# A transformer layer in split fp32 on one Trainium2 core: places and order of weight sums, two loads moved, a doubled half chunk

## The reference, cut to what matters

```python
mod = (silu(c) @ wmod).reshape(4, 6, 1, 1024)          # sa, ca, ga, sb, cb, gb
h = layernorm(x) * (1 + ca) + sa                       # x: 4 x 512 x 1024
x = x + ga * (h @ (weight * block_mask).T)             # attention stand-in, 1024 x 1024
h = layernorm(x) * (1 + cb) + sb
w1, w2, w3 = nf4_table[q] * scale                      # scale by 64 inputs
y = (silu(h @ w1.T) * (h @ w2.T)) @ w3.T               # hidden 2752 = 21 chunks of 128 and one of 64
x = x + gb * y
```

## Time and profile before

| what | value |
|---|---|
| median of 3 runs | 1547.49 us (1547.21 to 1549.31) |
| profiled execution | 1548.19 us, its span 1546.5 us |
| TensorE, VectorE, ScalarE busy | 97%, 73%, 61% of the span |
| DMA queue of SP | 67.8% of 16 engines |
| plain chunks, pass 1 | about 259 to 328 us, 332 to 702 us |
| pass 2, down projection | about 702 to 1123.5 us, 1123.5 to 1542.4 us |

### The profile page before, as it was taken

How to read it: one execution, slowest core, us unless ns; L and a number is a source line. 1 busy time by engine, 2 the same in 40 slices (tenths; PEclk the granted TensorE clock), 3 DMA queues, 4 the chain that set the end, 5 groups by cost and what they waited for, 6 DMA issues and landing times.

```text
span 1546.5 us, 19239 instructions
## 1 busy us (share of the span) xinstructions
PE 1498.0 (97%) x6984; PEld 1232.5 (80%) x6984; DVE 1133.5 (73%) x1751; ACT 942.6 (61%) x1091; POOL 5.5 (0%) x10
## 2 busy tenths in 40 slices
PE   4899999989999999999999999999899999999998
PEld 3687888777888888888888888888688888888887
DVE  5687786798888898888655565656665767956894
ACT  3465677799999999834868677782333433332320
POOL 0000000000000000000000000000000000000000
PEclk9999999999999999999999999999899999999999
DMA  9976444766666666655567777775686878857973
GB/s 366 367 262 232 155 141 154 248 209 228 222 214 205 217 211 198 202 187 178 188 207 243 229 230 238 232 229 192 227 303 251 313 235 309 324 172 269 400 275 119
DMA packets 188191, 362.78 MB, mean 235 GB/s; under 512 B 15392, under 2 KB 82368, under 8 KB 187072
## 3 DMA queue, kind: packets, MB, share of 16 engines
q1 hardware_dynamic: 181760, 358.39, 67.8%
q10 hardware_dynamic: 6336, 3.15, 0.7%
HBM read 258.16 MB, written 103.32 MB: 234 GB/s over the span
## 4 chain that ended last, share of the span: by engine, by line
PE 80%; DVE 8%; DMA 7%; ACT 2%; issue 2%; SPq 1%; DVEq 0%; ACTq 0%
PE ps L2290 15%; PE ps L2291 15%; PE ps L2292 15%; PE ps L2363 9%; PE ps L2361 9%; PE ps L2362 9%; PE ps L2196 2%; PE ps L2198 2%; PE ps L2197 2%; DMA weight_piece<-wT 1%; PE ps L2151 1%; DMA wmod<-wmod 1%; ACT w_raw L1046 1%; DMA xm_d<-modulated 1%; DMA x_d<-x_extra 1%
## 5 line engine op out<-in xcount | busy, mean ns | idle before, releaser
L2290 PE MATMUL ps<-x_m_hi,up_weight_hi 128*128 128x512 f32 x972 | 381.7, 393 | 15.4 <-ACT up_c L1276 7.2
L2291 PE MATMUL ps<-x_m_lo,up_weight_hi 128*128 128x512 f32 x972 | 380.6, 392 | 0.0
L2292 PE MATMUL ps<-x_m_hi,up_weight_lo 128*128 128x512 f32 x972 | 380.4, 391 | 0.0
L1046 ACT ACTIVATE w_raw<-w_raw 128x2048 f32<-128x2048 f32 (+1 forms) x145 | 271.9, 1875 | 3.5
L2361 PE MATMUL ps<-t_hi,s_hi 128*128 128x512 f32 x616 | 239.6, 389 | 0.0
L2362 PE MATMUL ps<-t_lo,s_hi 128*128 128x512 f32 x616 | 239.6, 389 | 0.0
L2363 PE MATMUL ps<-t_hi,s_lo 128*128 128x512 f32 x616 | 239.6, 389 | 0.0
L2290 PEld LDWEIGHTS ps<-x_m_hi,up_weight_hi 128*128 128x128 f32 x972 | 183.6, 189 | 55.8 <-DVE up_weight_lo L1507 10.3
L1369 ACT ACTIVATE s_hi<-s_raw 128x1408 fp32r<-128x1408 f32 x56 | 77.4, 1383 | 239.6 <-DVE s_raw L1986 191.6
L2292 PEld LDWEIGHTS ps<-x_m_hi,up_weight_lo 128*128 128x128 f32 x972 | 183.9, 189 | 38.7
L2291 PEld LDWEIGHTS ps<-x_m_lo,up_weight_hi 128*128 128x128 f32 x972 | 183.8, 189 | 37.7
(11 more groups left out here) (150 smaller groups left out, 1960.3 us busy)
## 6 DMA issues: line engine op xcount, KB each, us to landing
s_raw<-h_d SPq DMA_DIRECT2D x96, 704.0 KB, 5.7
up_weight_raw<-t_d SPq DMA_DIRECT2D x150, 256.0 KB, 5.2
wmod<-wmod SPq DMA_DIRECT2D x12, 2048.0 KB, 15.8
t_d<-up_weight_raw SPq DMA_DIRECT2D x91, 256.0 KB, 3.0
t_raw<-w_d SPq DMA_DIRECT2D x88, 256.0 KB, 6.4
w_codes<-w12q SPq DMA_DIRECT2D x41, 512.0 KB, 5.0
w_d<-w_raw SPq DMA_DIRECT2D x22, 512.0 KB, 3.9
t_raw<-w_d SPq DMA_DIRECT2D x22, 512.0 KB, 8.5
```

Source lines behind the costliest of these rows:

```text
L1046: act.activation(RAW2[n % 2][:, cols], RAW2[n % 2][:, cols] if j else RQ2[n % 2][:, cols], ACT.Prelu, bias=bias, scale=sign, alpha=slope). ...
L2290: pe.matmul(acc, th[:, k, :], xh[:, k, :], start=(first and k == 0), stop=False, skip_group_check=onto)
L2291: pe.matmul(acc, th[:, k, :], xl[:, k, :], start=False, stop=False, skip_group_check=onto)
L2292: last = pe.matmul(acc, tl[:, k, :], xh[:, k, :], start=False, stop=(stop and k == HALF_C - 1), skip_group_check=onto)
```

## The change

1. `TS` has eight places: 104 to 110 KB (the later place of `x_m3_hi`), 188, 190, 184 and 186 KB (the two `HM` places). The sums of chunk 1 are made first, then those of chunk 0, then 2. `TS_SLOT` says which place each takes; two places share a semaphore.
2. The decode of chunk 1 gets one more line before the modulation of tile 6; tile 7 goes to `HM[0]` and no longer waits for the store of tile 6. Stage blocks are loaded in another order.
3. VectorE: `finish` of chunk 1, sums of chunk 1, three sums of chunk 0, h of chunk 0, the other two sums. The low parts of x blocks m7 and m6 move behind the first weights of step 1, and `both_used` of step 0 behind `combine` of chunk 4. The raw block of m7 has a place of its own at 176 KB, so the rows for tiles 8 and 9 are loaded later, and `LN2_AT` is one step later.
4. ScalarE: lines of chunks 1, 3 and 4 are cut in other places; the copy of m2 of step 0 comes after all lines of chunk 4.
5. SP: in pass 2 the first scale and codes of w3 are issued behind three weights of the next step and not ahead of them. At its end, s of tile 0 and the first t chunks are issued behind the tail weights. The store of h of chunk 2, batch 1, moves behind the codes of chunk 5.
6. ScalarE at the end of pass 2: the copy of m4 and the SiLU of m3 come before t_hi of chunks 8 to 10.
7. Down projection, m4, m5 and m7: chunk 10 is loaded into both partition halves, the low part of s is made in the upper half of `SH`, the low part of t is zero there, and the third matmul of this chunk is left out.

```diff
-    TS = [at(f"combined_{i}", [HALF_C, P], F32, 184 + 2 * i) for i in range(4)]
+    TS = [at(f"combined_{i}", [HALF_C, P], F32, kb) for i, kb in enumerate((104, 106, 108, 110, 188, 190, 184, 186))]
...
+             "m7": at("x_m7_raw_first", [HALF_C, SEQ], F32, 176)[:]}
...
-    SUMS = [(n, name) for n in range(PLAIN) for name in SUM_NAMES]
+    SUMS = [(n, name) for n in (1, 0, 2) for name in SUM_NAMES]
+    TS_SLOT = (0, 1, 2, 3, 4, 5, 6, 7, 0, 1, 4, 5, 6, 7, 4)
...
-    LN2_AT = PLAIN + 1
+    LN2_AT = PLAIN + 2
...
-        return 1 if e < HALF_TILES else e % 2
+        return 1 if e < HALF_TILES - 1 else e % 2 if e >= HALF_TILES else 0
...
+    SHORT_K = [p[0] in ("m4", "m5", "m7") for p in PRODUCTS]
...
+                    if SHORT_K[m // JT]:
+                        sp.dma_start(SR[p][:, 1 - n, 0:HC - 1].rearrange("p c k -> p (c k)"),
+                                     h_d[tile * P:(tile + 1) * P, 0:(HC - 1) * P]).then_inc(s_raw_loaded[p], 16)
+                        for to in (0, TAIL):
+                            sp.dma_start(SR[p][to:to + TAIL, 1 - n, HC - 1],
+                                         h_d[tile * P:tile * P + TAIL, (HC - 1) * P:HC * P]).then_inc(s_raw_loaded[p], 16)
...
-            for name in SUM_NAMES:
-                store_sum(0, name)
...
                 load_codes(n + 2, 0)
                 load_codes(n + 2, 1)
+                if n == 1:
+                    for name in SUM_NAMES:
+                        store_sum(0, name)
...
                     if i < len(coming):
                         load_weight_up(*coming[i])
+                    if c == 1 and i == 2:
+                        sp.wait_ge(xs_added, len(X_SUMS))
+                        for name in ("m2", "m5"):
+                            sp.wait_ge(xc_lo, X_READY.index((1, name)) + 1)
+                        load_s3(0)
+                        for j in range(3):
+                            load_w3_codes(j)
...
-                if c == FULL - 2:
+                if c == FULL - 1:
                     for p in range(3):
                         sp.wait_ge(w3_stored[p], 16 * w3_uses(p))
                     load_s(0)
...
-            lines(4, 0, 5)
+            lines(4, 0, 4)
             silu(2, 1)
+            lines(4, 4)
+            copy_up(0, "m2")
             x_high(0, "m7")
-            lines(4, 5, 7)
-            copy_up(0, "m2")
-            lines(4, 7)
...
             silu_up(tail, 1)
-            for k in (8, 9):
+            copy_up(g, "m4")
+            silu_up(g, 1)
+            for k in (8, 9, 10):
                 t_high(0, k)
-            copy_up(g, "m4")
-            t_high(0, 10)
-            silu_up(g, 1)
...
-            sums(0, SUM_NAMES[:4])
             finish(1, 0)
-            sums(0, SUM_NAMES[4:])
             finish(1, 1)
-            sums(1, SUM_NAMES[:4])
+            sums(1, SUM_NAMES)
+            sums(0, SUM_NAMES[:3])
             make_h(0, 0)
             make_h(0, 1)
-            sums(1, SUM_NAMES[4:])
+            sums(0, SUM_NAMES[3:])
...
                 else:
+                    both_used(g)
                     for name in OPEN:
                         weight_sum(nxt, name)
                     split_up(nxt, OPEN)
+                    x_low(0, "m7")
+                    x_high_last()
+                    x_low(0, "m6")
...
+                if SHORT_K[m // JT]:
+                    dve.tensor_tensor(SH[p][TAIL:P, HC - 1, :], SR[p][TAIL:P, 1, HC - 1], SH[p][TAIL:P, HC - 1, :].bitcast(F32), ALU.subtract)
+                    dve.tensor_tensor(SL[p][:, 0:HC - 1], SR[p][:, 1, 0:HC - 1], SH[p][:, 0:HC - 1].bitcast(F32), ALU.subtract).then_inc(s_lo, 1)
...
-                    last = pe.matmul(acc, SL[p][:, k, :], TH[place(i)][k][:], start=False, stop=(k == HC - 1))
+                    short = SHORT_K[i] and k == HC - 1
+                    last = pe.matmul(acc, SH[p][:, k, :], TL[place(i)][k][:], start=False, stop=short)
+                    if not short:
+                        last = pe.matmul(acc, SL[p][:, k, :], TH[place(i)][k][:], start=False, stop=(k == HC - 1))
```

More of the change, by code:

```diff
@@ L503, in s_loads @@
     def s_loads(m):
-        return 16 * sum(len(PRODUCTS[n // JT][1]) for n in range(m % 4, m + 1, 4))
+        return 16 * sum(len(PRODUCTS[n // JT][1]) * (3 if SHORT_K[n // JT] else 1) for n in range(m % 4, m + 1, 4))
     def one_row(i):
@@ L513, in t_loads @@
     def t_loads(i, u):
-        return 16 * sum(len(UNITS[u]) * (1 if one_row(n) else len(PRODUCTS[n][3])) for n in range(i + 1))
+        return 16 * sum((len(UNITS[u]) + (SHORT_K[n] and HC - 1 in UNITS[u])) * (1 if one_row(n) else len(PRODUCTS[n][3]))
+                        for n in range(i + 1))
     C_OPS = {"m6": 0, "m2": 1, "m4": 3, "m1": 2, "m3": 3, "m5": 4, "m7": 3}
@@ L783, in load_t @@
                 for k in UNITS[u]:
-                    if one_row(i):
-                        row = ((blocks[0][0] - 1) * HC + k) * P
-                        sp.dma_start(TR[place(i)][k][:].rearrange("p a n -> p (a n)"), w3_d[row:row + P, :]).then_inc(t_raw_loaded[u], 16)
-                    else:
-                        for n, (half, d) in enumerate(blocks):
-                            row = ((half - 1) * HC + k) * P
-                            sp.dma_start(TR[place(i)][k][:, 1 - n, :], w3_d[row:row + P, (d - 1) * HALF:d * HALF]).then_inc(t_raw_loaded[u], 16)
+                    parts = [(0, TAIL), (TAIL, TAIL)] if SHORT_K[i] and k == HC - 1 else [(0, P)]
+                    for to, rows in parts:
+                        if one_row(i):
+                            row = ((blocks[0][0] - 1) * HC + k) * P
+                            sp.dma_start(TR[place(i)][k][to:to + rows].rearrange("p a n -> p (a n)"),
+                                         w3_d[row:row + rows, :]).then_inc(t_raw_loaded[u], 16)
+                        else:
+                            for n, (half, d) in enumerate(blocks):
+                                row = ((half - 1) * HC + k) * P
+                                sp.dma_start(TR[place(i)][k][to:to + rows, 1 - n, :],
+                                             w3_d[row:row + rows, (d - 1) * HALF:d * HALF]).then_inc(t_raw_loaded[u], 16)
             def finish_w3(j):
@@ L860, in _ @@
                 codes_after(c + 1)
+                if c == PLAIN:
+                    for d in range(2):
+                        load_normed(d)
                 if c == FULL - 2:
@@ L1233, in _ @@
             act.wait_ge(early_line, NL * 2 + 3)
-            lines(1, 3, 4)
+            lines(1, 3, 5)
             modulate_again(HALF_TILES - 2)
@@ L1293, in silu_up @@
                     act.activation(UG[0][:], UG[0][:], ACT.Silu).then_inc(silu_done, 1)
-            lines(1, 4)
+            lines(1, 5)
             silu(0, 0)
@@ L1300, in _ @@
             silu(1, 0)
-            lines(3, 0, 4)
+            lines(3, 0, 5)
             for name in ("m1", "m4", "m3"):
@@ L2001, in t_low @@
                 dve.wait_ge(t_hi, i * HC + k + 1)
-                dve.tensor_tensor(TL[place(i)][k][:], TR[place(i)][k][:, 1, :], TH[place(i)][k][:].bitcast(F32), ALU.subtract).then_inc(t_lo, 1)
+                rows = P
+                if SHORT_K[i] and k == HC - 1:
+                    rows = TAIL
+                    dve.memset(TL[place(i)][k][TAIL:P, :].bitcast(F32), 0.0)
+                dve.tensor_tensor(TL[place(i)][k][0:rows, :], TR[place(i)][k][0:rows, 1, :], TH[place(i)][k][0:rows, :].bitcast(F32),
+                                  ALU.subtract).then_inc(t_lo, 1)
             def t_units(i, units):
```

101 lines of the change are left out of this document (53 added, 48 removed).

## The result

The changed kernel takes **1538.87 us**, median of 4 runs (1537.4 to 1541.86), against 1547.75 of the kernel before on the same chip, 8.9 us less by the medians. The ratio over all runs is 0.995, 95% interval 0.9937 to 0.9963, which would be 7.7 us less (5.7 to 9.8). Forecast were 1531.3 and 16.2 us less. The direction was right and the time lies inside the range of 1524 to 1541, but only about half of the gain came. The profiled execution took 1539.52 us, and its span fell from 1546.5 to 1537.8.

What follows compares the result with a forecast made beforehand. TensorE bounds the kernel, busy 1498.0 of 1546.5 us. Gains 2.7 + 10.1 + 0.8 + 2.6 = 16.2 us give span 1530.3, time 1532.0, and 1531.3 us as the median is 0.7 below the profiled run; range 1524 to 1541.

Steps and rivals of the forecast that it cites:

- Part 1: Half chunk in m4, m5, m7: 5.4 us of matmuls dropped, 2.7 given back in m5, worth 2.7 us.
- The term of VectorE: In m5: the changed subtractions for s_lo cost +0.07 us a tile; VectorE alone gives back 0.8 us.
- The DMA term: In m5: small transfers make the DMAs 0.65 us a tile later, over three tiles 1.9 us.
- The price of a packet: Small rows of s in m5: 49 ns a packet, less 21 ns for its 512 bytes.
- Rivals C and D: m5: C, 100 ns a packet, 8 us stalls, 1537 to 1541, chance 0.10; D, 141 ns, 20.7 us, 1552.9, chance 0.04.
- Part 2: End of the second pass: the 7.2 us gap before m7 and 3.0 us of slow clock go, 10.1 us.
- rival B: End of the pass only moves its gap, or tile 1 waits; 5 to 7 us lost, 1537; chance 0.12.
- Part 3: Second pass: w3's codes and scale behind three weights remove a stall at the copy of m2, 0.8 us.
- Part 4: Plain chunks and first steps: stalls mostly change places, 2.6 us of gain remain, range 0 to 8.
- rival A: Plain chunks: VectorE's two waits for stores really go, gaps near 331 and 351 close, about 8 us gained, 1526; chance 0.15.
- The step that failed: Step 1: m3 meets both_used, ready at 366.7, and starts at 367.7 us, against 370.7 before.
- The second step that failed: Turn-over of the passes: the turn one step later still leaves 18 us before pass 2 reads its stage blocks.

Runs made afterwards that it cites:

- one_load: The changed kernel with each block of s fetched by one transfer in place of three, a small part of the result left out; 1537.01 us.
- plain_undone: The changed kernel with all edits to the plain chunks, steps 0 and 1 and the turns taken back; 1535.87 us.
- end_scalar_only: The kernel before with only ScalarE's copy of m4 and SiLU of m3 put ahead of t chunks 8 to 10; 1540.85 us.
- normed_later: The changed kernel with the two loads of normed rows one step later, behind the codes of step 1's next chunk; 1535.74 us.

## Why the prediction was right and wrong, step by step

**Part 1, half chunk: 1.6 us, not 2.7.** The 5.44 us of matmuls went; 3.8 us came back and not 2.7. The term of VectorE was mis-sized. I took +0.07 us a tile for the short operation: it lasts 0.29 us and its neighbour gets 0.13 shorter, and in the back-to-back stretch a tile goes from 8.52 to 8.81 us, +0.29. The DMA term was the other way round: 1.9 us expected, about 1.0 by one_load. Put into the sum of the prediction, 7 x 0.29 and 1.0 give 1.6 + 2.0 + 1.0 - 1.2 = 3.4 of the 3.8 us; 0.3 more are waits in the first two tiles of m7, of which the prediction has none. The price of a packet was right, though. From 1423 to 1475 us the queues of the changed kernel and of one_load show (packets, MB, share of 16 engines over 52 us):

```profile
q1 hardware_dynamic: 7779, 19.09, 103.7%
```

```profile
q1 hardware_dynamic: 5866, 19.56, 99.3%
```

That is 863 and 826 us of engine time. At one_load's pace 19.09 MB take 806 us and 5725 packets; the 2054 packets more cost 57 us, 28 ns each over their bytes, as the 49 - 21 ns of the prediction. What was too high is the step from there to the stall. The prediction let the DMAs' lateness grow over three tiles, but in the later tiles VectorE no longer waits for data (its last wait over 0.5 us is at 1425.97 in the changed kernel, at 1441.43 before), so only the later of the two would count there. That fits the rows, but was not tried by itself. Rivals C and D are out: waits in the last three tiles of m5 and the first two of m7, not in every tile. The Trainium skill advises against two transfers to disjoint partition halves (DMA: Bandwidth & Descriptors, Rules for kernel authors), since both run on the same engines and gain nothing over one; the prediction took that for a loss, and the trace shows next to none, with 28 ns a packet and about 1.0 us of stalls in all. The fixed 2 us of that page, from which the prediction estimated 8 us a tile, are given there for DMAs issued by gpsimd; these are issued by SP.

**Part 2, end of pass 2: 10.25 us of 10.1.** The most valuable step, the copy of m4 ahead of t_hi, held, for the reason given: with the copy ahead, m7 follows at once. But part of that is luck. Alone the edits are worth 8.1 us, since tile 1 then waits for s_lo; this is the thin margin of which the prediction warned (0.8 us), and rival B in a small form. s_lo of tile 1 starts 5.52 us after the down projection in the changed kernel, which is in time by 0.3 us, and 6.07 to 7.04 us after it in eight others, each of which waits there (*down* 0.4 to 1.4 us, apart from m5): I put that down to when the last t chunks land, which no run tried. And of the two edits that I costed as one, SP's was not needed for the gap, by the one trace of each.

**Part 3, w3: 0.8 us or more.** *turn-over* is 1.07 before and 0 in plain_undone. In end_scalar_only the same stall was 2.40 us, with 1.7 of slow clock: my upper bound of 0.8 was one execution's value. Of the four kernels without part 3 each has 1.07 to 4.25 us there.

**Part 4, plain chunks: 2.6 us of gain forecast, 3.3 of loss measured** (71.71 + 12.07 + 6.56 + 2.00, less 73.02 + 9.59 + 6.44 and less the 0 that part 3 leaves of 1.07). The forecast's 2.6 was not quite what its own numbers give, 370.7 - 367.7 - 0.85 = 2.2. By stretch, against 2.2 us of gain forecast in *plain* 1.3 came, *step 0-1* lost 2.5 where next to nothing was expected, and *turn-over* lost 2.0 where nothing was. In order:
- VectorE's wait for the decode, 2.2 us, and its waits for places, 3.2 + 4: measured 2.21, 4.16 and 3.46 (the two waits for places in the order in which they come, 7.6 us in sum for 7.2). x sums began at 296.30, only 0.35 before; taken from the first plain group the shift of m1 of step 0 is 1.3 us, and 1.8 on average. That term was about right, and rival A was wrong.
- The gap at m1 of step 0: 3.5 us expected, 3.1 found, but its slow clock cost 2.9 us and not 1.8.
- No wait at m3 of step 0 nor at m1 of step 1: right.
- The gap before m7 of step 0 on the copy of m4: 4.1 us expected from 353.6 on, 2.2 found before 358.5, without slow clock.
- **The step that failed:** "m3 of step 1 then meets both_used of step 1 [...] and starts at 367.7". It started at 372.64 (the start of m4 at 368.26, 2.72 us of matmuls and 1.67 of slow clock). In the way stood m4 of step 1, which waits for the copy of m2, and I never placed this copy. It stands behind two lines of chunk 6, whose codes SP asks for at 356.8 only. I had followed ScalarE's list up to the copy that I was looking for and not to the next; and I moved the loads of normed rows without pricing them where they land, which made these codes about 1 us later. The gap of 4.0 us with its 1.7 of slow clock is this step's.
- **The second step that failed:** "The turn one step later still leaves 18 us before pass 2 reads its stage blocks." The 18 us were there: the last turn's rows were stored from 660.26 on, and VectorE was ready for the blocks at 678.2. What I didn't ask is which transfers these loads then meet, and I put the cost at nothing: it was 2.0 us here, 4.2 on average.

**Chance.** 1.0 us of the missing gain in the profiled pair is the start-up. That *turn-over* was 2.0 us in it, the lowest of six, is luck. The misses add up to the 7.5 us between forecast and span: 1.1 (part 1), 5.9 (part 4) and 1.0, less 0.15 and 0.27 for parts 2 and 3.

## What to carry to other kernels

When an edit moves an engine ahead, follow every consumer on each in-order list for two whole steps, not only to the first gap you find: what is gained at one wait is taken at the next entry that has not moved. For each transfer that moves, ask what else is in the queue where it lands; two moves whose data were in time by themselves cost about 1 and 4 us here by making others late, the first with slow clock on top. And count stalls against the pace of the bounding engine, stretch by stretch: that told apart effects of 1 to 3 us which the medians of whole runs, with stretches that vary by 2 to 4 us, could not.

## What the runs showed of the hardware

**The price of a gap is not fixed.** In the 14 profiles TensorE had 36 gaps of 2.3 to 7.2 us after 275 us. After 32 of them the matmuls that followed lost 1.5 to 3.1 us to the lower clock level, most of them near 1.7 or near 2.9; after four (2.6, 2.7, 3.1 and 3.1 us long) nothing over 0.15. The granted clock of the traces says the same: between 275 us and the last matmul it fell to 1.2 GHz 32 times, at these 32 gaps and at no shorter one. What decides whether it falls is open. The same gap of 3.1 us at m1 of step 0 cost 1.8 before, 2.9 in the changed kernel and 0.1 in normed_later. Shorter gaps, of up to 2.2 us, cost 0.2 at most. I had taken 1.8 us as if it were a constant. That it is the clock is seen in stretches of the profile; the changed kernel had a granted clock of 0.56 in the 5 us around its gap (the third number from the end):

```profile
330.00:335.00 5.00, 3.54 (x8) 2.82 (x9) 4.97 (x11) 4.97 (x4) 0.00 (x0) 0.56 0.43 145
```

and normed_later, after the same gap:

```profile
328.00:333.00 5.00, 4.57 (x20) 3.79 (x21) 4.94 (x9) 4.94 (x5) 0.00 (x0) 1.00 0.26 82
```

**A small operation costs more than its columns.** 64 x 128 elements took 0.29 us on VectorE, while 128 columns fewer in an operation of 128 x 1408 saved 0.13. Where VectorE works without a pause, leaving the small one out shortened a tile by 0.43 us (8.81 to 8.38). Half the partitions saved nothing: the subtraction for t_lo lasts 0.69 us with 64 x 512 (at 1477.47 in the changed kernel) and with 128 x 512.

**Small packets** cost 28 ns of one engine's time over their bytes, the same on a queue at 103.7% with large ones as the estimate from the stretch of small ones had given. Of the 2054 more, about 1670 are rows of 512 bytes and the rest smaller; the trace does not part the two.
